# Two mixture routers: a quarter of the side matrices on GpSimd, and group scores through a small network of maxima and minima

## The chip, the cores and the metric

The kernel runs on one core of a Trainium2 chip. The metric is the device time of one execution in microseconds (us). The kernel before was timed three times: 1511.66, 1504.87 and 1511.73 us, median 1511.66 us. One further execution was profiled.

A core has five engines that run their own instruction streams and meet at semaphores: TensorE (PE, with its weight loads as PEld), VectorE (DVE), ScalarE (ACT), GpSimd (POOL) and SyncE (SP, which here only issues DMAs).

## The reference

A two-layer network on 2048 tokens (64 sequences of 32) of width 256. Layer 0: cross attention over a context of 257 rows with 16 heads, a gated linear recurrence (log-space cumulative sums), and a mixture of 8 experts. Layer 1: cross attention, causal self attention, and a mixture of 16 experts. Each part is added to `x` after a layer norm of its input.

The change touches only how the two mixtures choose and place their tokens:

- first mixture: softmax over 8 logits of a token, its 2 best experts;
- second mixture: `sb = sigmoid(logits) + bias` over 16 experts in 4 groups of 4. A group's score is the sum of its two best `sb`; the 2 best groups stay allowed, and the 4 best experts in them are taken.

Then each chosen expert's two-layer network runs on the tokens that chose it, and the weighted results are added to the token.

## The kernel before, in words

Tokens lie as 16 tiles (`NT`) of 128 rows. The program is a row of blocks; at the end of each, all engines meet (a drain and a semaphore exchange, line 1101 in the profile, where the block of a router ends). For each mixture there is: a layer norm block (`boundary`), which also writes the normalised rows to DRAM and computes the logits; the router (`route`, lines 1094 to 1224), called once for each mixture; then the expert tiles (`first_tiles`, `second_tiles`).

`route` makes a table: for each of the NTL tiles of 128 expert rows (39 in the first mixture, 79 in the second) which token stands in each row. In its block:

1. `choose` (on DVE): the scores are ranked. In the second mixture it is the function in `route_second`, lines 2298 to 2332. It takes all six pairs of a group's four `sb` (six additions, line 2306, 64 columns each), and their running maximum (five operations, line 2310, each waiting for the one before); then come the groups' ranks (lines 2317 on) and the 8 best experts (`top8`).
2. Counting (DVE, two matmuls): from the one-hot choices, each token's place within its expert, and from these its row, split into its low 7 bits `lo_f` and a tile threshold `hi_f` (lines 1166 to 1207). All of it is one chain on DVE, nearly every step waiting for the one before.
3. The placing loop (lines 1133 to 1138, 1145 to 1149, 1209 to 1214). It has K times 16 units (32 in the first mixture, 64 in the second). For a unit `u`, DVE makes `hot_lo` (128x128, f16): a row's column is compared with `lo_f` and multiplied by the token's number (tensor_scalar with two operands per partition). ACT makes `side` (128 x NTL+1, f16): the Sign of the column's number plus `hi_f`, so -1 before the tile and +1 from it on. PE multiplies the two and adds up over the 16 units of a choice in PSUM. Both matrices have a ring of 8 buffers; a maker of unit `u` waits until PE has placed unit `u`-8 (`m_placed`), and PE waits for `m_onehot` and `m_side` of its unit.
4. The end: ACT halves the sums (line 1151), DVE subtracts neighbouring columns, which leaves the token's number in its tile alone, and writes `r.token`.

POOL has no instruction in the router's block before the change. SP issues the fetch of the remaining expert weights there (line 980). POOL's next work is in the block behind: gathers of token rows by `r.token` (`gather`, lines 1443 and 1682); the second mixture issues 44 of them (R-4) ahead of its first scatter.

## Time and profile before

| what | us |
|---|---|
| median of three runs | 1511.66 |
| lowest, highest | 1504.87, 1511.73 |
| profiled execution, its own time | 1497.39 |
| its span (first to last instruction) | 1495.6 |
| PE, DVE, ACT, POOL busy | 1160.9, 1026.2, 822.4, 436.4 |
| granted TensorE clock, mean share | 0.889 |
| first router's block, DVE from 539.88 to 558.92 | 19.0 |
| second router's block, DVE from 1109.35 to 1151.13 | 41.8 |

The profiled execution stands 14.3 us under the median of the runs. 1.8 us of its time lie outside the span. PE is the busiest engine over the whole, but a share over the whole says little of a stage: in the routers' blocks PE waits most of the time. In a row of the timeline a merged piece "x64" has the start of the first and the time from there to the end of the last.

### The profile page before, as it was taken

The numbers are of one execution on the slowest core, as the hardware profiler recorded it, in microseconds if no ns is written. First come the engines' busy times: TensorE is split into PE (matmuls) and PEld (weight loads), VectorE is DVE, ScalarE is ACT, GpSimd is POOL, SyncE is SP. The second block draws the span as 40 slices with busy tenths as digits, with TensorE's granted clock in tenths as the row PEclk, the third lists the DMA queues.
The fourth block names the chain that finished last, engine by engine and source line by source line (L and its number), as shares of the span: only waits on it lengthen the run. The fifth ranks groups of instructions, "written<-read, shape, count | busy, mean of one in ns | idle before, by whom it ended". The sixth has DMA issues, their size and how long they took to land. (4 is left out here: it accounts for less than half of the span.)

```text
span 1495.6 us, 41196 instructions
## 1 busy us (share of the span) xinstructions
PE 1160.9 (78%) x13430; PEld 857.0 (57%) x13430; DVE 1026.2 (69%) x2880; ACT 822.4 (55%) x2156; POOL 436.4 (29%) x480
## 2 busy tenths in 40 slices
PE   4899999998699549999999936877936137777780
PEld 2688787886446439988888723334722124555560
DVE  5699999997746888966666545544587168455466
ACT  6688888886588567844443406116455144444450
POOL 0555555552110000023333201100201721555650
PEclk9999999999899759999999967988955578999995
DMA  3333333332000266011111159980063310222228
GB/s 97 97 81 78 81 81 78 82 78 61 23 1 0 70 256 251 2 62 48 48 52 52 38 175 343 315 273 25 1 229 144 102 37 22 80 73 75 81 71 286
DMA packets 111935, 151.45 MB, mean 101 GB/s; under 512 B 13632, under 2 KB 96960, under 8 KB 111680
## 3 DMA queue, kind: packets, MB, share of 16 engines
q1 hardware_dynamic: 95792, 114.11, 24.3%
q0 software_dynamic: 11328, 30.95, 6.6%
q10 hardware_dynamic: 4688, 4.72, 1.0%
q8 instruction: 78, 1.28, 0.4%
q14 instruction: 49, 0.40, 0.1%
HBM read 127.97 MB, written 21.76 MB: 100 GB/s over the span
## 5 line engine op out<-in xcount | busy, mean ns | idle before, releaser
L1359 ACT ACTIVATE mixture_and_attentions_h<-ps,mixture_and_attentions_b 128x128 f32<-128x128 f32 x440 | 124.8, 372 | 136.7 <-PE ps L1307 132.5
L1307 PE MATMUL ps<-xture_and_attentions_m_w 128*128 128x128 f16 x1872 | 155.7, 219 | 1.7 <-DVE xture_and_attentions_m_w L1387 1.7
L1307 PEld LDWEIGHTS ps<-xture_and_attentions_m_w 128*128 x1872 | 129.1, 98 | 36.4 <-issue 2.9
L679 POOL TENSOR_TENSOR ads_and_recurrence_ctx_s<-ads_and_recurrence_ctx_c,ads_and_recurrence_ctx_s 128x512 f16<-128x512 f32 x64 | 74.1, 1158 | 177.7 <-ACT ads_and_recurrence_ctx_s L608 177.7
L1325 PE MATMUL ps<-xture_and_attentions_m_w,ixture_and_attentions_hs 128*128 x312 | 117.4, 379 | 1.0 <-DVE xture_and_attentions_m_w L1413 1.0
L628 ACT ACTIVATE ads_and_recurrence_probs<-ps,s_and_recurrence_neg_max 128x257 f32<-128x257 f32 x256 | 117.6, 479 | 1.1 <-DVE s_and_recurrence_neg_max L710 1.1
L1686 POOL DMA_INDIRECT y_rows<-stage_second_mixture_y,ge_second_mixture_r_dest x79 | 77.1, 975 | 128.8 <-DVE stage_second_mixture_y L1648 115.2
L1682 POOL DMA_INDIRECT tage_second_mixture_rows<-n_rows,e_second_mixture_r_token x79 | 77.1, 975 | 111.6 <-POOLq L1101 87.8
L1443 POOL DMA_INDIRECT ture_and_attentions_rows<-n_rows,e_and_attentions_r_token x39 | 39.2, 1006 | 240.9 <-POOLq L1101 142.4
L1550 PE MATMUL ps<-stage_second_mixture_m_w,stage_second_mixture_x_s 128*128 x474 | 95.1, 339 | 15.7 <-issue 7.1
L1395 DVE TENSOR_SCALAR ixture_and_attentions_hs<-mixture_and_attentions_h 128x512 f16<-128x512 f32 x110 | 47.5, 432 | 81.2 <-PE ps L1326 70.5
L1627 DVE SCALAR_TENSOR_TENSOR stage_second_mixture_h<-ps,stage_second_mixture_h 128x192 f32<-128x192 f32 x95 | 33.7, 355 | 98.1 <-ACT stage_second_mixture_h L1599 60.6
L1565 PE MATMUL ps<-stage_second_mixture_m_w,stage_second_mixture_h_t 128*128 (+1 forms) x95 | 27.0, 285 | 78.0 <-DVE x_sb L1644 36.2
L719 DVE TENSOR_SCALAR _heads_and_recurrence_pn<-ads_and_recurrence_probs,heads_and_recurrence_inv 128x256 f32<-128x256 f32 x256 | 79.7, 371 | 8.3
L1326 PE MATMUL ps<-xture_and_attentions_m_w,ixture_and_attentions_hs 128*128 x312 | 85.0, 273 | 0.0
L710 DVE TENSOR_REDUCE s_and_recurrence_neg_max<-ps 128x2 f32<-128x514 f32 x128 | 81.9, 678 | 1.2 <-PE ps L550 1.2
L525 PE MATMUL ps<-ads_and_recurrence_ctx_s,currence_wh_L_xattn_wk_t 128*128 128x256 f16 x512 | 78.3, 276 | 5.2 <-issue 5.2
L1599 ACT ACTIVATE stage_second_mixture_h<-ps 128x192 f32<-128x192 f32 x95 | 31.5, 331 | 92.3 <-PE ps L1550 45.4
L1397 DVE SCALAR_TENSOR_TENSOR ixture_and_attentions_hs<-mixture_and_attentions_h,ixture_and_attentions_hs 128x512 f16<-128x512 f32 x110 | 76.3, 693 | 3.8
L558 PE MATMUL ps<-consts_sb,_heads_and_recurrence_pn 128*128 128x128 f32 x512 | 77.0, 273 | 2.2 <-DVE heads_and_recurrence_p_t L726 2.2
L534 PE MATMUL ps<-currence_wh_L_xattn_wv_t,ads_and_recurrence_ctx_s 128*128 128x256 f16 x512 | 77.3, 274 | 0.0
L1447 POOL DMA_INDIRECT y_rows<-xture_and_attentions_m_w,re_and_attentions_r_dest x39 | 38.4, 985 | 131.5 <-DVE xture_and_attentions_m_w L1413 131.2
(408 smaller groups left out, 3355.0 us busy)
## 6 DMA issues: line engine op xcount, KB each, us to landing
ads_and_recurrence_ctx_t<-in_ctx_t SPq DMA_DIRECT2D x64, 257.0 KB, 2.7
e_and_attentions_b_ctx_t<-in_ctx_t SPq DMA_DIRECT2D x15, 1028.0 KB, 9.3
ure_and_attentions_b_ctx<-in_ctx SPq DMA_DIRECT2D x30, 512.0 KB, 8.6
xture_and_attentions_m_w<-in_m_w SPq DMA_DIRECT2D x2, 5632.0 KB, 37.9
ds_and_recurrence_mask_i<-in_mask SPq DMA_DIRECT2D x256, 32.1 KB, 1.7
tage_second_mixture_rows<-y_rows SPq DMA_DIRECT2D x16, 512.0 KB, 9.6
stage_second_mixture_m_w<-in_m_w SPq DMA_DIRECT2D x2, 3840.0 KB, 19.3
xture_and_attentions_m_w<-in_m_w SPq DMA_DIRECT2D x1, 5120.0 KB, 15.4
```

Of the source, the lines that this page charges most:

```text
L525: last = pe.matmul(ps[:, KB, m * KR:(m + 1) * KR], w[:, c, m * P:(m + 1) * P], x[:, c, :], start=(n_ == 0), stop=(n_ == len(products) - 1))
L534: last = pe.matmul(ps[:, VB, r * D:(r + 1) * D], x[:, c, r * P:(r + 1) * P], w[:, c, :], start=(n_ == 0), stop=(n_ == len(products) - 1))
L628: act.activation(probs[p][:, j, :], ps[:, SB + j, 0:SK], ACT.Exp, bias=neg_max[:, p, j:j + 1], accum_out=sums[:, p, j:j + 1]).then_inc(k.a ...
L710: dve.tensor_reduce(neg_max[:, p, 2 * h:2 * h + 2], ps[:, SB + 2 * h:SB + 2 * h + 2, 0:SK], AX.X, ALU.max, negate=True).then_inc(k.a_max.s ...
L719: last = dve.tensor_scalar(pn[p][:, j, :], probs[p][:, j, 0:KR], inv[:, p, j:j + 1], None, ALU.mult)
L1307: last = pe.matmul(ps[:, UB + 2 * (u % 2) + f // PER, (f % PER) * P:(f % PER + 1) * P], slots.of(e, c, at, P), a[:, c, :], start=(n == 0), ...
L1325: pe.matmul(ps[:, YB + u % 2, 0:2 * D], h, slots.of(e, block, at, 2 * D), start=(f == 0), stop=False)
L1326: last = pe.matmul(ps[:, YB + u % 2, 0:D], l, slots.of(e, block, at, D), start=False, stop=(f == FC - 1))
L1359: last = act.activation(h32[n][:, at:at + P], ps[:, UB + 2 * (u % 2) + n, at:at + P], ACT.Silu, scale=1 / (WS * NS), bias=b1[:, bass.ds(e ...
L1550: last = pe.matmul(ps[:, UB + u % 2, 0:UP], a[:, c, :], weight(u, w, c * UP, UP), start=(n == 0), stop=(n == len(products) - 1))
L1682: pool.indirect_dma_start(rows[s % R][:, :], None, k.n_rows, bass.IndirectOffsetOnAxis(ap=r.token[:, s:s + 1], axis=0)).then_inc(k.t_rows[ ...
L1686: pool.indirect_dma_start(k.y_rows, bass.IndirectOffsetOnAxis(ap=r.dest[:, s:s + 1], axis=0), y[s % Y], None).then_inc(k.t_stored[s % Y].s ...
```

## The change

- In the placing loop, units 3, 7, 11, ... (a quarter: 8 of 32, 16 of 64) get their `side` from POOL instead of ACT, as 0 or 1 instead of -1 or +1: `(column + hi_f) > 0`, a tensor_scalar with one operand per partition. Their `hot_lo` is multiplied by twice the token's number instead, so that the later halving still fits. A new small table `twice` (16 columns) is made on DVE ahead of `choose`. PE waits for `m_fourth` on these units.
- In `choose` of the second mixture, the 6 additions and 5 maxima become 2 operations of 128 columns (maxima and minima of the first and the second two of a group), 3 of 64 columns, and 2 more of 64 columns, each waiting for the one before; there are 4 waits instead of 6.
- The semaphore `m_counted` is gone; its one increment goes to `m_known`, whose later thresholds rise by one. No other order changes.

```diff
+        twice = k.sb("twice", [P, NT], ctx=ctx)
+        def of_pool(u):
+            return u % 4 == 3
...
-                    pe.wait_ge(k.m_side.sem, k.m_side.at(u + 1))
+                    if of_pool(u):
+                        pe.wait_ge(k.m_fourth.sem, k.m_fourth.at(u // 4 + 1))
+                    else:
+                        pe.wait_ge(k.m_side.sem, k.m_side.at(u + 1 - u // 4))
...
+                    if of_pool(u):
+                        continue
                     act.wait_ge(k.m_placed.sem, k.m_placed.at(u - AHEAD + 1))
                     act.activation(side[u % AHEAD][:, :], iota_h[:, 0:NTS], ACT.Sign, bias=hi_f[:, kk, t:t + 1]).then_inc(k.m_side.sem, 1)
...
+        @block.gpsimd
+        def _(pool):
+            pool.wait_ge(k.m_known.sem, k.m_known.at(2))
+            for u in range(3, K * NT, 4):
+                kk, t = divmod(u, NT)
+                pool.wait_ge(k.m_placed.sem, k.m_placed.at(u - AHEAD + 1))
+                pool.tensor_scalar(side[u % AHEAD][:, :], iota_h[:, 0:NTS], hi_f[:, kk, t:t + 1], 0.0, ALU.add, ALU.is_gt).then_inc(k.m_fourth.sem, 1)
...
+            dve.tensor_scalar(twice[:, :], c_["token"], 2.0, None, ALU.mult)
             choose(dve)
...
-                    dve.tensor_scalar(hot_lo[u % AHEAD][:, :], iota_h[:, :], lo_f[:, kk, t:t + 1], c_["token"][:, t:t + 1], ALU.is_equal, ALU.mult).then_inc(k.m_onehot.sem, 1)
+                    dve.tensor_scalar(hot_lo[u % AHEAD][:, :], iota_h[:, :], lo_f[:, kk, t:t + 1], twice[:, t:t + 1] if of_pool(u) else c_["token"][:, t:t + 1], ALU.is_equal, ALU.mult).then_inc(k.m_onehot.sem, 1)
...
-            pairs = [(a, b) for a in range(EG) for b in range(a + 1, EG)]
-            for n, (a, b) in enumerate(pairs):
-                last = dve.tensor_tensor(pair[:, n, :, :], sb[:, :, :, a], sb[:, :, :, b], ALU.add)
-            last.then_inc(k.m_chain.sem, 1)
-            dve.wait_ge(k.m_chain.sem, k.m_chain.next())
-            for n in range(1, len(pairs)):
-                dve.tensor_tensor(pair[:, 0, :, :], pair[:, 0, :, :], pair[:, n, :, :], ALU.max).then_inc(k.m_chain.sem, 1)
-                dve.wait_ge(k.m_chain.sem, k.m_chain.next())
+            first, second = sb[:, :, :, 0:2], sb[:, :, :, 2:4]
+            dve.tensor_tensor(more[:, :, :, :], first, second, ALU.max)
+            dve.tensor_tensor(less[:, :, :, :], first, second, ALU.min).then_inc(k.m_chain.sem, 1)
+            dve.wait_ge(k.m_chain.sem, k.m_chain.next())
+            dve.tensor_tensor(pair[:, 1, :, :], more[:, :, :, 0], more[:, :, :, 1], ALU.min)
+            dve.tensor_tensor(pair[:, 2, :, :], less[:, :, :, 0], less[:, :, :, 1], ALU.max)
+            dve.tensor_tensor(pair[:, 3, :, :], more[:, :, :, 0], more[:, :, :, 1], ALU.max).then_inc(k.m_chain.sem, 1)
+            dve.wait_ge(k.m_chain.sem, k.m_chain.next())
+            dve.tensor_tensor(pair[:, 4, :, :], pair[:, 1, :, :], pair[:, 2, :, :], ALU.max).then_inc(k.m_chain.sem, 1)
+            dve.wait_ge(k.m_chain.sem, k.m_chain.next())
+            dve.tensor_tensor(pair[:, 0, :, :], pair[:, 3, :, :], pair[:, 4, :, :], ALU.add).then_inc(k.m_chain.sem, 1)
```

## Rows read from the trace of the kernel before

**Rows 1.** The page's first part: busy time, share, instructions of each engine.
```profile
PE 1160.9 (78%) x13430; PEld 857.0 (57%) x13430; DVE 1026.2 (69%) x2880; ACT 822.4 (55%) x2156; POOL 436.4 (29%) x480
```
**Rows 2.** Windows: stretch, length, busy (PE, PEld, DVE, ACT, POOL), clock, DMA share, GB/s.
```profile
550.40:558.00 7.60, 6.49 (x32) 3.33 (x32) 7.21 (x32) 7.14 (x33) 0.00 (x0) 0.50 1.02 409
1132.60:1149.20 16.60, 14.40 (x64) 6.68 (x64) 14.92 (x64) 16.21 (x64) 0.00 (x0) 0.50 0.04 14
```
**Rows 3.** Timeline, second router, scores: start, length, engine, line, operation.
```profile
1110.98 0.42 DVE L2301 TENSOR_TENSOR age_second_mixture_sbias<-stage_second_mixture_y,ixture_w_L_ffn_gate_bias 128x256 f32<-128x256 f32 x1 [1.15 <-ACT stage_second_mixture_y L2296]
1111.44 1.17 DVE L2306 TENSOR_TENSOR tage_second_mixture_pair<-age_second_mixture_sbias 128x64 f32<-128x64 f32 x6
1112.65 1.26 DVE L2310 TENSOR_TENSOR tage_second_mixture_pair<-tage_second_mixture_pair 128x64 f32<-128x64 f32 x5
1113.94 0.42 DVE L2317 TENSOR_TENSOR tage_second_mixture_rank<-tage_second_mixture_pair 128x256 f32<-128x256 f32 x1
```
**Rows 4.** Timeline, second router, the whole placing loop on ACT and DVE.
```profile
1132.61 16.21 ACT L1149 ACTIVATE tage_second_mixture_side<-ge_second_mixture_iota_h,tage_second_mixture_hi_f 128x80 f16<-128x80 f16 x64 [21.56 <-DVE tage_second_mixture_hi_f L1207]
1132.61 14.92 DVE L1214 TENSOR_SCALAR ge_second_mixture_hot_lo<-ge_second_mixture_iota_h,tage_second_mixture_lo_f,consts_sb 128x128 f16<-128x128 f16 x64
```
**Rows 5.** Timeline, the same loop: DVE in its first and last units.
```profile
1132.61 1.65 DVE L1214 TENSOR_SCALAR ge_second_mixture_hot_lo<-ge_second_mixture_iota_h,tage_second_mixture_lo_f,consts_sb 128x128 f16<-128x128 f16 x7
...
1146.71 0.82 DVE L1214 TENSOR_SCALAR ge_second_mixture_hot_lo<-ge_second_mixture_iota_h,tage_second_mixture_lo_f,consts_sb 128x128 f16<-128x128 f16 x3
```
**Rows 6.** Timeline, first router: scores, counting, placing loop, the next block's start.
```profile
540.15 0.28 DVE L1793 TENSOR_SCALAR ixture_and_attentions_lg<-ps 128x128 f32<-128x128 f32 x1
...
545.18 0.29 DVE L1169 TENSOR_TENSOR xture_and_attentions_tmp<-xture_and_attentions_hot 128x128 f32<-128x128 f32 x1
545.51 0.23 DVE L1174 CAST ure_and_attentions_any_h<-xture_and_attentions_tmp 128x128 f16<-128x128 f32 x1
...
547.00 0.17 DVE L1182 TENSOR_SCALAR re_and_attentions_need_i<-ture_and_attentions_upto 128x8 int32<-128x8 f32 x1
...
550.38 7.08 ACT L1149 ACTIVATE ture_and_attentions_side<-re_and_attentions_iota_h,ture_and_attentions_hi_f 128x40 f16<-128x40 f16 x32 [4.05 <-DVE ture_and_attentions_hi_f L1207]
550.39 7.23 DVE L1214 TENSOR_SCALAR re_and_attentions_hot_lo<-re_and_attentions_iota_h,ture_and_attentions_lo_f,consts_sb 128x128 f16<-128x128 f16 x32
...
559.23 6.98 PE L1307 MATMUL ps<-n,xture_and_attentions_m_w 128*128 128x128 f16 x93 [1.34 <-PEq L1101]
```
**Rows 7.** Groups by shape, POOL: busy us, mean ns | idle before.
```profile
L673 POOL TENSOR_SCALAR ds_and_recurrence_mask_b<-ds_and_recurrence_mask_i 128x257 bf16<-128x257 int32 x64 | 70.1, 1096 | 5.4
L672 POOL TENSOR_TENSOR ads_and_recurrence_q_blk<-heads_and_recurrence_q_t,consts_sb 128x128 f32<-128x128 f32 x64 | 29.1, 455 | 0.0
...
L2144 POOL TENSOR_TENSOR x_sb<-x_sb,d_attentions_w_L_attn_bv 128x256 f32<-128x256 f32 x16 | 11.0, 726 | 111.4 <-SPq L2140 111.4
```
**Rows 8.** Single lines, DVE tensor_scalar forms: min/median/max ns, first and last start.
```profile
L2226 DVE TENSOR_SCALAR ture_and_attentions_c_pn<-e_and_attentions_c_probs,ure_and_attentions_c_inv x16: 277/278/845, 1055.3 to 1081.0; 128x128 f32<-128x128 f32 x16
...
L719 DVE TENSOR_SCALAR _heads_and_recurrence_pn<-ads_and_recurrence_probs,heads_and_recurrence_inv x256: 332/342/571, 52.0 to 363.8; 128x256 f32<-128x256 f32 x128
...
L343 DVE TENSOR_SCALAR ads_and_recurrence_ln_xn<-x_sb,s_and_recurrence_ln_mean,ads_and_recurrence_ln_sd x32: 395/397/412, 9.5 to 402.5; 128x256 f32<-128x256 f32 x32
...
L1214 DVE TENSOR_SCALAR ge_second_mixture_hot_lo<-ge_second_mixture_iota_h,tage_second_mixture_lo_f,consts_sb x64: 303/308/316, 1132.6 to 1147.2; 128x128 f16<-128x128 f16 x64
```
**Rows 9.** Timeline, DVE's tensor_scalar of line 2226 beside POOL's bias additions.
```profile
1054.63 2.78 POOL L2144 TENSOR_TENSOR x_sb<-x_sb,d_attentions_w_L_attn_bv 128x256 f32<-128x256 f32 x4
...
1055.28 0.84 DVE L2226 TENSOR_SCALAR ture_and_attentions_c_pn<-e_and_attentions_c_probs,ure_and_attentions_c_inv 128x128 f32<-128x128 f32 x1
```
**Rows 10.** Timeline behind the second router: first and last of the 44 gathers, PE.
```profile
1152.06 0.99 POOL L1682 DMA_INDIRECT tage_second_mixture_rows<-n_rows,e_second_mixture_r_token  x1 [87.83 <-POOLq L1101]
...
1206.66 0.95 POOL L1682 DMA_INDIRECT tage_second_mixture_rows<-n_rows,e_second_mixture_r_token  x1 [0.30 <-issue]
...
1214.31 0.40 PE L1565 MATMUL ps<-stage_second_mixture_m_w,stage_second_mixture_h_t 128*128 128x256 f16 x1 [32.21 <-DVE x_sb L1644]
```

More of the change, by code:

```diff
@@ L1143, in _ @@
             act.activation(warm[:, :], k.ident_h[:, 0:1], ACT.Sign)
-            act.wait_ge(k.m_known.sem, k.m_known.at(1))
+            act.wait_ge(k.m_known.sem, k.m_known.at(2))
             for kk in range(K):
@@ L1221, in _ @@
             dve.tensor_scalar(r.token[:, :], row_f[:, :], 1.0, 0.0, ALU.subtract, ALU.max)
-    for s, n in ((k.m_logits, 1), (k.m_counted, 1),
-                 (k.m_prefixed, 1), (k.m_onehot, NT * K), (k.m_placed, NT * K), (k.m_side, NT * K), (k.m_halved, 1), (k.m_shift, 1), (k.m_expd, 1)):
+    for s, n in ((k.m_logits, 1),
+                 (k.m_prefixed, 1), (k.m_onehot, NT * K), (k.m_placed, NT * K), (k.m_side, NT * K - NT * K // 4), (k.m_fourth, NT * K // 4), (k.m_halved, 1), (k.m_shift, 1), (k.m_expd, 1)):
         s.base += n
@@ L1351, in silu @@
                 if u == NT:
-                    act.wait_ge(k.m_known.sem, k.m_known.at(2))
+                    act.wait_ge(k.m_known.sem, k.m_known.at(3))
                 e = mix.E if u < NT else routed.of(u - NT)
@@ L1450, in _ @@
                 gather(s)
-            pool.wait_ge(k.m_known.sem, k.m_known.at(3))
+            pool.wait_ge(k.m_known.sem, k.m_known.at(4))
             for s in range(mix.tiles):
@@ L1467, in first_tiles @@
         k.t_rows[b].base += (mix.tiles + R - 1 - b) // R
-    k.m_known.base += 3
+    k.m_known.base += 4
     slots.finish()
@@ L1582, in _ @@
                 if u + 4 == NT:
-                    pe.wait_ge(k.m_known.sem, k.m_known.at(2))
+                    pe.wait_ge(k.m_known.sem, k.m_known.at(3))
                 if u + 4 >= NT:
@@ L1693, in _ @@
                 if s == 0:
-                    pool.wait_ge(k.m_known.sem, k.m_known.at(3))
+                    pool.wait_ge(k.m_known.sem, k.m_known.at(4))
                 scatter(s)
@@ L2284, in route_second @@
         sb = k.sb("sbias", [P, NT, NG, EG], ctx=ctx)
-        pair = k.sb("pair", [P, 6, NT, NG], ctx=ctx)
+        pair = k.sb("pair", [P, 5, NT, NG], ctx=ctx)
+        more, less = (k.sb(n, [P, NT, NG, 2], ctx=ctx) for n in ("more", "less"))
         rank = k.sb("rank", [P, 3, NT, NG * NG], ctx=ctx)
@@ L2439, in build @@
         k.m_logits = k.count("m_logits")
-        k.m_counted = k.count("m_counted")
         k.m_prefixed = k.count("m_prefixed")
@@ L2444, in build @@
         k.m_side = k.count("m_side")
+        k.m_fourth = k.count("m_fourth")
         k.m_known = k.count("m_known")
```

10 lines of the change are left out of this document (5 added, 5 removed).

## The prediction

> **What bounds the kernel now.** I read the page's busy shares first [rows 1]: PE is busy 78% of the span, so most stages are PE's, but the change lies in the two stretches where PE hardly works. There I took the windows [rows 2] and then the timeline of each router.
>
> The second router's block is a chain on DVE up to the placing loop. The scores begin at 1110.98, after DVE has waited 1.15 us for ACT, and pass through the six additions and five maxima to the ranks at 1113.94 without a gap [rows 3]. So each microsecond saved there is one saved on the path.
>
> In the placing loop three engines run in step: the question is which sets the pitch. In the second router ACT's 64 units take 16.21 us: less the last one's 0.35, over 63 steps, a pitch of 0.252 us. DVE's 64 take 14.92 [rows 4], and that is not one pitch: its first seven take 1.65, so (1.65 - 0.31)/6 = 0.223 us, its last three 0.82, so 0.253 us [rows 5]. DVE runs ahead until its ring of 8 is full, and from there goes at the pace of PE, which goes at ACT's. ACT is the bound, DVE has 0.029 us a unit to spare. In the first router ACT's matrix is only 40 wide: ACT (7.08 - 0.31)/31 = 0.218 us, DVE (7.23 - 0.31)/31 = 0.223 us [rows 6]. There DVE is the bound already, and taking work from ACT frees nothing.
>
> What follows each router takes a shift whole. PE starts at 559.23 behind the first, with 93 matmuls in one piece [rows 6]. Behind the second POOL issues 44 gathers from 1152.06 to 1207.6, and PE, after 32.21 us of idle time, goes on only at 1214.31 [rows 10]. I read this long stall as tied to the burst of gathers, whose start is the router's end: it moves with the router and hides nothing. A fixed point in it that would swallow a gain, such as the landing of the weights fetched at the block's start, I don't see: the loop's window shows the DMA engines 4% busy [rows 2], so the 9 MB asked for before it have landed.
>
> **The change, part by part.** The sum is made against the profiled execution: span 1495.6, its time 1497.39.
>
> *Scores of the groups (second router only).* Removed: from 1111.44 to 1113.94, 2.50 us [rows 3]. Added: two operations of 128 columns. The pitch of independent 64-column ones is (1.17 - 0.26)/5 = 0.18 us [rows 3], with 64 more columns about 0.25; one that the next waits for costs 0.33 at 128 columns (545.18 to 545.51 [rows 6]). So 0.25 + 0.33 = 0.58. Three of 64 columns: 0.18 + 0.18 + 0.29 = 0.65. Two in a chain at the pitch of line 2310, (1113.94 - 1112.65)/5 = 0.26 us: 0.52. Sum 1.75, a saving of 0.75 us. Bounds: 0.55, if pairs of adjacent columns cost what awkward operands do, and 0.9.
>
> *The table `twice`.* In the second router DVE has 1.15 us of idle time there, so nothing. In the first, `choose` starts at 540.15 with no wait ahead of it: 16 columns at most the 0.17 us of line 1182, back to back rather less: +0.1 us [rows 3, 6].
>
> *ACT's quarter moved.* ACT does 3 units of 4, 3 x 0.252 = 0.76 us per four, under DVE's 4 x 0.223 = 0.89. If POOL's share cost nothing, the second router's loop would be DVE's: 63 x (0.252 - 0.223) = 1.8 us less. The first: nothing.
>
> *What POOL's operation costs.* Its form is not in the trace. POOL's tensor_tensor takes 0.455 us at 128 columns and 0.726 at 256, a slope of 2.1 ns and 0.19 fixed; its only tensor_scalar takes 1.10 at 257 columns, with the same fixed part 3.5 ns a column [rows 7]. For 80 columns that is 0.36 or 0.47, for 40 columns 0.27 or 0.33; the ceiling is the whole 1.10. I take 0.47 and 0.33, by the row of its own kind. POOL has 0.89 us for each, and may begin when the unit 8 before is placed, 1.8 us ahead of need. So POOL itself is in time, also for unit 63, which is POOL's and the last.
>
> *What POOL's operation does to DVE.* This decides the sign. DVE's tensor_scalar of line 2226 takes 0.278 us in the median of 16, and up to 0.845 in those beside POOL's bias additions [rows 8]. In one, DVE's starts at 1055.28 and lasts 0.84, until just after the POOL operation that began 0.03 later has ended (POOL's pitch there is (2.78 - 0.73)/3 = 0.68) [rows 9]. So this kind of DVE operation stands still while POOL runs, and `hot_lo` is of this kind: 256 columns of float32 cost 64 ns more than 128 (0.342 against 0.278), half of what they cost a tensor_tensor (0.42 against 0.29 [rows 3, 6]), and a second operand per partition 55 ns more (0.397). By these a 128-column float32 form with two operands would take 0.333; `hot_lo`, in f16, takes 0.308, so it goes at that double rate or a higher one [rows 8]. How much a POOL operation of length d takes from DVE: where it begins just behind DVE's, 0.845 - 0.278 = 0.57 of 0.72, so d - 0.155. Where it begins anywhere in DVE's period of 0.223 us, a part of that lies beside DVE's own work: on the mean over the period about half of 0.223 less, d - 0.27; and the start and end of a short one, which hold nothing, weigh more, so I take d - 0.30. That is 0.17 us at d = 0.47 and 0.03 at 0.33.
>
> *Sum of the loops.* Second router: 63 x 0.223 = 14.05 for DVE alone, plus 15.75 x 0.17 = 2.7, makes 16.7, against 15.9 (63 x 0.252) before: +0.9 us. The break-even is 0.115 us per POOL operation. First: 7.75 x 0.03 = +0.2 us. All together: +0.9 + 0.2 + 0.1 - 0.75 = **+0.4 us**, 0.03%.
>
> The Trainium skill, "SBUF — State Buffer", section "SBUF: two separate sides", says that VectorE in a mode that uses both of its ports and GpSimd take a shared port pair as an exclusive lock, held for the whole instruction, the other being blocked entirely. The stretched rows of line 2226 agree in kind (0.278 to 0.845 [rows 8]). Read to the letter, the rule gives rival C at its full length, +7.5 us; the row shows 0.57 lost of 0.72.
>
> **The rivals.**
>
> *A, the wash (forecast):* as above, -1 to +2 us.
>
> *B, POOL lies beside DVE at no cost.* For it: most POOL and DVE operations in the trace overlap without a change; a POOL operation of 0.36 us could fit in the gaps between DVE's. Then -1.8 + 0.1 - 0.75 = -2.4 us. Against it: [rows 8, 9].
>
> *C, the slower side: each POOL operation stops DVE for most of its length.* Place: `hot_lo` in both loops; price: d - 0.155, so 0.315 and 0.175 us, for DVE always has the next one waiting. It decides from 0.115 us on. 15.75 x (0.893 + 0.315) - 15.9 = +3.1 us, first router 7.75 x 0.175 = +1.4, with the rest +3.9 us. If DVE loses all of POOL's length, 15.75 x 0.47 + 7.75 x 0.33 = 10.0 us stand in place of A's 2.9: +7.5 us. If POOL's operation costs the ceiling of 1.10, DVE's four and POOL's one in turn give 4 x 0.223 + 1.10 - 0.16 = 1.83 us per four: +13 us in the second, +7.3 in the first, +19.6 in all. I give this far end little.
>
> *D, the burst behind the second router falls otherwise.* PE comes out of it at 1214.31, 6.7 us behind the last gather's issue [rows 10]. I don't know what delays it, so a shift against it can let a tile more or fewer through. PE's idle piece of 32.21 us longer or shorter by a tenth or two is 3 to 6 us either way.
>
> The change doing less than it says is in A and C: in the first router it takes work from an engine that isn't the bound.
>
> **How the numbers follow.** Chances: A 0.47, B 0.18, C 0.23 (0.05 of it DVE losing all of POOL's length, 0.03 the far end), D 0.12. But for those two parts of C, all are below 0.5% of the time (7.5 us), about what a measurement of this kernel can tell from no change, since its own three runs lie 0.45% apart. To this I add that the medians themselves may wander by as much: faster 0.20, same 0.61, slower 0.19. The time: the median 1511.66 + 0.4 is 1512.1. The other executions seen, 1504.87 and 1497.39, lie below, none above 1511.73, so the next median is rather lower: I take 1511.0. The range: upwards C's 3.9 and some of its upper parts, or D, over 1511.7, 1520; downwards B or D from the lower runs (1504.87 - 2.4, less a part of the way to 1497.4), 1499.
>
> **What would show it.** The six-and-five group replaced by 1.75 us, the ranks starting 0.75 earlier. In the second loop: ACT's pieces with gaps (no longer the bound), DVE's `hot_lo` with one in four stretched by about 0.17 us, POOL's operations 0.47 long at a pitch of 1.06, the loop about 16.7 us on DVE. The first loop 7.1 us instead of 6.9. B shows as `hot_lo` at 0.308 throughout and a loop of 14 us; C as stretched ones of 0.62 and a loop over 18 us. The burst must still last 55.6 us and PE resume 62 us after its start; if not, D. The prediction is wrong if POOL's operation lasts near 1 us, if ACT's start waits for POOL's ring, or if the whole moves by over 0.5% by something outside both routers.

## The result: 3 to 4 us faster, and the profile after

The changed kernel takes 1499.92 us in the median of 16 executions (1478.22 to 1503.76), the kernel before 1503.87 beside it (16 executions, 1500.40 to 1511.73): 3.95 us less. The ratio of the comparison is 0.993, 95% interval 0.9904 to 0.9956. Forecast was 1511.0 with 0.61 on no difference. The ratio shows a larger gain than the medians (3.95 us are 0.26%), because it leaves out executions more than 1.5% above the lowest of their kernel: two of the changed kernel's came out near 1480, so its seven over 1500.4 fall away, and none of the kernel before. The medians are the better guide.

The page of the profiled execution after (1502.55 us, span 1500.8), first part:

```profile
span 1500.8 us, 41196 instructions
PE 1168.7 (78%) x13430; PEld 859.3 (57%) x13430; DVE 1027.1 (68%) x2878; ACT 818.8 (55%) x2132; POOL 452.3 (30%) x504
```

Against [rows 1], ACT has 24 instructions fewer (8 and 16 side matrices) and POOL 24 more. This execution is longer than the profiled one of before, 1495.6, although both routers' stretches together are shorter: the first router begins 3.5 us later than before and the second another 3.4, nearly all of it in work that the change doesn't touch (0.3 of the 3.4 is the first router's own). Two single profiles can't be subtracted; stretches of them can.

Windows of the two placing loops after, which answer to [rows 2]:

```profile
554.00:561.80 7.80, 6.72 (x32) 3.33 (x32) 7.38 (x32) 5.84 (x25) 3.61 (x8) 0.50 1.03 411
1138.50:1153.50 15.00, 14.19 (x64) 6.65 (x64) 14.48 (x65) 13.14 (x49) 9.74 (x16) 0.50 0.11 43
```

The scores, on DVE, answering to [rows 3]:

```profile
1117.89 0.42 DVE L2321 TENSOR_TENSOR age_second_mixture_sbias<-stage_second_mixture_y,ixture_w_L_ffn_gate_bias 128x256 f32<-128x256 f32 x1 [1.07 <-ACT stage_second_mixture_y L2316]
1118.35 0.29 DVE L2325 TENSOR_TENSOR tage_second_mixture_more<-age_second_mixture_sbias 128x128 f32<-128x128 f32 x1
1118.55 0.28 DVE L2326 TENSOR_TENSOR tage_second_mixture_less<-age_second_mixture_sbias 128x128 f32<-128x128 f32 x1
1118.87 0.23 DVE L2328 TENSOR_TENSOR tage_second_mixture_pair<-tage_second_mixture_more 128x64 f32<-128x64 f32 x1
1119.02 0.22 DVE L2329 TENSOR_TENSOR tage_second_mixture_pair<-tage_second_mixture_less 128x64 f32<-128x64 f32 x1
1119.15 0.21 DVE L2330 TENSOR_TENSOR tage_second_mixture_pair<-tage_second_mixture_more 128x64 f32<-128x64 f32 x1
1119.40 0.22 DVE L2332 TENSOR_TENSOR tage_second_mixture_pair<-tage_second_mixture_pair 128x64 f32<-128x64 f32 x1
...
1119.92 0.43 DVE L2341 TENSOR_TENSOR tage_second_mixture_rank<-tage_second_mixture_pair 128x256 f32<-128x256 f32 x1
```

From `sbias` to the ranks it is 2.03 us instead of 2.96: -0.93. From start to start, the first of 128 columns costs 0.20, the second 0.32, and the three of 64 columns 0.15, 0.13 and 0.25.

The single lines of `hot_lo` on DVE and of the side matrices on POOL after (min/median/max ns, first and last start), which answer to [rows 8]:

```profile
L1233 DVE TENSOR_SCALAR ge_second_mixture_hot_lo<-ge_second_mixture_iota_h,tage_second_mixture_lo_f,consts_sb x48: 296/298/328, 1138.6 to 1152.5; 128x128 f16<-128x128 f16 x48
...
L1233 DVE TENSOR_SCALAR ge_second_mixture_hot_lo<-ge_second_mixture_iota_h,tage_second_mixture_lo_f,age_second_mixture_twice x16: 296/298/354, 1139.3 to 1152.7; 128x128 f16<-128x128 f16 x16
```
```profile
L1173 POOL TENSOR_SCALAR tage_second_mixture_side<-ge_second_mixture_iota_h,tage_second_mixture_hi_f x16: 551/612/617, 1138.6 to 1151.6; 128x80 f16<-128x80 f16 x16
L1173 POOL TENSOR_SCALAR ture_and_attentions_side<-re_and_attentions_iota_h,ture_and_attentions_hi_f x8: 437/448/537, 554.0 to 559.9; 128x40 f16<-128x40 f16 x8
```

POOL's operation is longer than priced (0.61, not 0.47 us), and `hot_lo` hardly feels it: median 0.298 us, the worst 0.354. In the loop's first two groups of four and then in its steady state the timeline shows this:

```profile
1138.64 1.15 POOL L1173 TENSOR_SCALAR tage_second_mixture_side<-ge_second_mixture_iota_h,tage_second_mixture_hi_f 128x80 f16<-128x80 f16 x2 [67.49 <-DVE tage_second_mixture_hi_f L1226]
1139.25 0.35 DVE L1233 TENSOR_SCALAR ge_second_mixture_hot_lo<-ge_second_mixture_iota_h,tage_second_mixture_lo_f,age_second_mixture_twice 128x128 f16<-128x128 f16 x1
...
1141.82 0.61 POOL L1173 TENSOR_SCALAR tage_second_mixture_side<-ge_second_mixture_iota_h,tage_second_mixture_hi_f 128x80 f16<-128x80 f16 x1 [0.28 <-PE ps L1146]
1142.01 0.30 DVE L1233 TENSOR_SCALAR ge_second_mixture_hot_lo<-ge_second_mixture_iota_h,tage_second_mixture_lo_f,age_second_mixture_twice 128x128 f16<-128x128 f16 x1
1142.23 0.74 DVE L1233 TENSOR_SCALAR ge_second_mixture_hot_lo<-ge_second_mixture_iota_h,tage_second_mixture_lo_f,consts_sb 128x128 f16<-128x128 f16 x3
1142.71 0.61 POOL L1173 TENSOR_SCALAR tage_second_mixture_side<-ge_second_mixture_iota_h,tage_second_mixture_hi_f 128x80 f16<-128x80 f16 x1 [0.28 <-PE ps L1146]
1142.90 0.30 DVE L1233 TENSOR_SCALAR ge_second_mixture_hot_lo<-ge_second_mixture_iota_h,tage_second_mixture_lo_f,age_second_mixture_twice 128x128 f16<-128x128 f16 x1
```

From one `hot_lo` of POOL's units to the next it is 0.89 us, four steps of 0.223: DVE's free pace, with POOL at work in 0.61 of each 0.89. POOL's stretch of waiting (0.28 us, for PE) says that it isn't the bound. The loop, from the start of PE's first matmul to the start of its last, takes 13.99 us instead of 15.85: -1.86. The first router's takes 7.02 instead of 6.81: +0.21. `twice` costs 0.08 (543.635 to 543.712, the next operation's start). From `sbias` to gather 0 the second router takes 38.33 us instead of 41.08, -2.75. So the stretches give -2.75 + 0.21 + 0.08 = **-2.5 us**, where rival B said -2.4.

### The profile page after: what moved, and what is told of

Read it like the earlier page. It is cut to its first block and busy times, and to the rows that moved or that the text cites. A ratio compares the mean times of both kernels' runs of the same rounds, so it can differ in the third digit from the quotient of the medians.

```text
span 1500.8 us, 41196 instructions
## 1 busy us (share of the span) xinstructions
PE 1168.7 (78%) x13430; PEld 859.3 (57%) x13430; DVE 1027.1 (68%) x2878; ACT 818.8 (55%) x2132; POOL 452.3 (30%) x504
## 5 line engine op out<-in xcount | busy, mean ns | idle before, releaser
L1613 ACT ACTIVATE stage_second_mixture_x_s<-ps 128x512 f16<-128x512 f16 x79 | 47.3, 599 | 46.7 <-PE ps L1557 36.5
## 6 DMA issues: line engine op xcount, KB each, us to landing
xture_and_attentions_m_w<-in_m_w SPq DMA_DIRECT2D x1, 5120.0 KB, 15.6
```

## The experiments

Theory: the change is worth what its stretches show (-2.5 us), since POOL's operation costs DVE next to nothing. Rivals: the larger ratio is real and comes from what lies behind the router; POOL does stop DVE, and something hides it.

**The parts alone, the change and the kernel before once more.** Four kernels on one chip, the kernel before beside them (median 1498.92 us, 35 executions). The loops alone keep the six additions and five maxima:

```diff
-            first, second = sb[:, :, :, 0:2], sb[:, :, :, 2:4]
-            dve.tensor_tensor(more[:, :, :, :], first, second, ALU.max)
...
+            for n, (a, b) in enumerate(pairs):
+                last = dve.tensor_tensor(pair[:, n, :, :], sb[:, :, :, a], sb[:, :, :, b], ALU.add)
...
```

> The placing loops of the change alone, the group scores as before. Path theory (what a router saves is what the kernel saves): second loop, first to last matmul, 14.0 us instead of 15.9, first loop 7.0 instead of 6.8, group scores 2.95 as before; time 1.7 us under before, 0.1%. Burst theory (the change also alters how the 44 gathers' stall falls, and that gives the executions near 1480): single executions 15 to 25 us under the rest appear here too if POOL's new instructions are the cause.

The scores alone are the reverse.

> The network of maxima and minima alone, all side matrices on ACT. Path theory: 0.9 us from the first score to the ranks less than before, loops as before, time 0.9 us less. Burst theory: executions near 1480 only if a shift of the router's end, or another number of DVE instructions, is the cause; none if POOL's instructions are.

> The changed kernel once more. Path theory: median 2.6 us under before (router 2: 0.9 + 1.9, router 1: 0.2 back), 0.17%. Burst theory: again some executions (2 or 3 of 16) near 1480, and the mean 5 us or more under before; if there are none here, those seen were chance of the chip and not of the change.

> A copy of the kernel before, to see how far two sets of executions of one program differ. Both theories: median within 1.5 us of before's. If it shows executions near 1480 as well, these belong to both kernels. Its second trace tells how much the stretch from the second router's end to the last of 17 weight casts (91.0 us in the first trace) wanders by itself: under 1 us if it is set by the gathers alone, several if PE's stall in it is a matter of chance.

Later the change, the loops alone and the scores alone ran again, with the kernel before at 1504.82 (35 executions).

> The changed kernel, unaltered. One of two surroundings is possible: one in which the kernel before takes 1495 to 1505 us and PE pauses through the second mixture, or the one of the last four runs, in which it takes 1406.8 us and PE is full there. In either, the theory that the change is worth what its own stretches show (second loop -1.86, scores -0.93, first loop +0.2) expects -2.6 us: about 1404.2 beside 1406.8, or 1498 beside 1500.5, ratio 0.998. The rival, that the -10 us in the ratio of the first comparison is real and comes from what the mixture does with an earlier or later start, expects -8 to -12 us, 0.993.

> The kernel before with the part of the change in the loops alone (the scores as before). Own stretches: second loop -1.86, first loop +0.2, so -1.7 us. Rival: that this part by itself makes runs near 1475 us (4 of 12 in the first look), by 20 us, expects those again wherever the kernel before takes about 1500; where it takes 1407 there is no pause to lose, and both theories say -1.7.

> The kernel before with the network of the scores alone. Own stretch: -0.93 us (2.03 instead of 2.96 from sbias to rank). If that is all, the whole is 1 us less, within what can be told from nothing. Rival (what the router gives is lost behind it): 0.

Measured (medians in us; stretches from each kernel's profile):

```
                       median  beside before    sbias to ranks  loop 2  sbias to gather 0  loop 1
kernel before (trace)                             2.96          15.85      41.08            6.81
loops alone            1494.35     -4.57          2.96          14.00      39.27            7.04
loops alone, again     1500.32     -4.50          2.96          13.97      39.24            7.05
scores alone           1499.99     +1.07          2.04          15.85      40.16            6.81
scores alone, again    1505.10     +0.28          2.04          15.85      40.17            6.81
the change, again      1496.24     -2.68          2.03          14.01      38.36            7.03
the change, third      1501.16     -3.66          2.04          13.97      38.32            7.04
before, again          1500.45     +1.53          2.96          15.85      41.10            6.81
```

These stretches repeat to 0.05 us and add up: each part does what it does alone. The medians don't: the loops alone gain 3.0 us more than their stretches (1.5), twice, and the scores come out 1.2 to 2.0 worse than theirs (0.9). The kernel before against itself is off by 1.53 (one of those twelve executions took 1850.14 us; without it the median is 1500.42), so one such difference means little. That the loops came out alike twice stays open: the second time no execution lay apart, and the ratio, 0.9962 with an interval of 0.9943 to 0.9982, leaves out the 0.999 that their stretches give.

What wanders lies outside the routers. From gather 0 to the last scatter the two traces of the kernel before take 305.7 and 296.1 us, and from gather 0 to the last weight cast 91.0 and 79.4; the expectation had asked for under 1 us if the gathers alone set that stretch. The traces of the change and its parts beside them lie between 299 and 308 us. So ten microseconds can come and go there in one unaltered kernel, which is what rival D feared, and more than it priced (3 to 6).

A group of executions near 1475 us adds to the wander: 8 of the 88 of all kernels with a part of the change, none of the 98 of the kernel before (lowest 1489.82); none lies between 1481.38 and 1489.82. No profile fell on one of them. Their cause isn't known.

**Does POOL stop DVE?** In the kernel before, a two-input operation of POOL beside the loops, whose result nobody reads:

```diff
+        spare = k.sb("spare", [P, NT * K // 4 + 1, NTS], F16, ctx=ctx)
...
+        @block.gpsimd
+        def _(pool):
+            pool.wait_ge(k.m_known.sem, k.m_known.at(1))
+            for u in range(3, K * NT, 4):
+                pool.wait_ge(k.m_placed.sem, k.m_placed.at(u - AHEAD + 1))
+                pool.tensor_tensor(spare[:, u // 4, :], iota_h[:, 0:NTS], iota_h[:, 1:NTS + 1], ALU.subtract)
```

> The kernel before, with one thing added: in the loop over 0/1 matrices GpSimd subtracts, at every fourth step, two slices of iota_h (128x40 in the first router, 128x80 in the second, two fp16 inputs) into a tile that nobody reads. Nobody waits for it and ACT still makes every side matrix, so whatever it does to DVE's hot_lo is the pair's doing alone. If two-input operations of GpSimd are what stops DVE (the theory, from L2226 stretched beside a tensor_tensor in rows 8 and 9, while the one-input operation of the change left hot_lo at 0.297 us): the hot_lo that lies beside one is stretched by about as much as the GpSimd operation lasts, 0.4 to 0.6 us, four steps of DVE take 0.9 + 0.4 to 0.6 = 1.3 to 1.5 us against ACT's 1.0, and the second loop lasts 20 to 24 us instead of 15.85; whole time +5 to +8 us with both routers. If a short DVE operation on fp16 isn't stopped by GpSimd whatever that reads: hot_lo stays under 0.35 us, the loop lasts 15.9 us, whole time within 1 us.

Measured: 1406.13 against 1406.77 (that these are some 95 us lower is taken up below), ratio 1.0003 (0.9987 to 1.002). The single lines and the loop on ACT:

```profile
L1222 DVE TENSOR_SCALAR ge_second_mixture_hot_lo<-ge_second_mixture_iota_h,tage_second_mixture_lo_f,consts_sb x64: 298/302/433, 1133.7 to 1149.6; 128x128 f16<-128x128 f16 x64
L1159 POOL TENSOR_TENSOR age_second_mixture_spare<-ge_second_mixture_iota_h x16: 319/320/321, 1133.8 to 1148.4; 128x80 f16<-128x80 f16 x16
1133.73 16.21 ACT L1150 ACTIVATE tage_second_mixture_side<-ge_second_mixture_iota_h,tage_second_mixture_hi_f 128x80 f16<-128x80 f16 x64 [21.56 <-DVE tage_second_mixture_hi_f L1215]
```

One `hot_lo` that is held, by itself, and the POOL operation beside it:

```profile
1143.31 0.41 DVE L1222 TENSOR_SCALAR ge_second_mixture_hot_lo<-ge_second_mixture_iota_h,tage_second_mixture_lo_f,consts_sb 128x128 f16<-128x128 f16 x1
1143.35 0.32 POOL L1159 TENSOR_TENSOR age_second_mixture_spare<-ge_second_mixture_iota_h 128x80 f16<-128x80 f16 x1 [0.68 <-PE ps L1139]
```

The time went as the second theory had it, the operation as the first, if by 0.11 us and not 0.4 to 0.6: DVE stands until POOL's two-input operation is through. All 16 held ones of the second router end 0.047 to 0.050 us after POOL's operation, as all six stretched ones of line 2226 in the trace before [rows 8, 9] end 0.084 to 0.086 after theirs. So the price isn't fixed. The next `hot_lo` starts 0.031 us ahead of POOL's end, and the loss is POOL's length plus its start behind `hot_lo`'s, less 0.254: 0.114 where POOL (0.320) begins 0.048 behind, 0.131 where it begins 0.065 behind, 0.044 beside the first, 0.256 us long, of the first router. Five of the first router's eight (0.253 us) begin 0.21 behind a `hot_lo`, end in time for the next, and cost nothing.

Why doesn't the loop feel it? The steady state's four steps are 3 x 0.223 + 0.337 = 1.006 us, and ACT's are 4 x 0.252 = 1.007. My reading, not tested, is that this is no accident: POOL's start is released by PE, which goes at ACT's pace, so if DVE gets ahead, POOL starts later behind `hot_lo` and holds it longer. The loop stays at 15.85 and the total doesn't move. ACT's slack hides the loss here; beside a loop that DVE bounds, as the changed one, a two-input operation was not tried.

**POOL without rest: every second matrix.** `u % 2 == 1` in place of `u % 4 == 3`, and the counts to match.

> The changed kernel with GpSimd making every second side matrix instead of every fourth. DVE at 0.223 us a step is what bounds the changed loop (13.99 us for 63 steps in the second router). If GpSimd's own pace is the limit of sharing: its operation takes 0.61 us with some 0.05 us until the next, two steps take 0.66 us, the second loop lasts 31 x 0.66 = 20 to 21 us and the first, with 0.45 us an operation, about 16 x 0.5 = 8 us; whole time +6 to +8 us over the changed kernel. If GpSimd stops DVE more, the more of its time it works, DVE's hot_lo is stretched too, above 0.35 us for most. If GpSimd had kept pace, both loops would stay at 14.0 and 7.0 us and the whole within 1 us.

Measured 1407.82 against 1406.77 (+1.05; ratio 0.9999 to 1.0024). Single lines, second router:

```profile
L1233 DVE TENSOR_SCALAR ge_second_mixture_hot_lo<-ge_second_mixture_iota_h,tage_second_mixture_lo_f,consts_sb x32: 305/312/317, 1134.9 to 1151.3; 128x128 f16<-128x128 f16 x32
L1233 DVE TENSOR_SCALAR ge_second_mixture_hot_lo<-ge_second_mixture_iota_h,tage_second_mixture_lo_f,age_second_mixture_twice x32: 308/389/394, 1135.2 to 1151.6; 128x128 f16<-128x128 f16 x32
L1173 POOL TENSOR_SCALAR tage_second_mixture_side<-ge_second_mixture_iota_h,tage_second_mixture_hi_f x32: 544/547/607, 1135.0 to 1151.6; 128x80 f16<-128x80 f16 x32
```

The loop takes 16.84 us, not 20: back to back POOL's operation is 0.547 long and its pitch 0.533. Every second `hot_lo` is 0.39 long and its step 0.310, 0.087 lost. The first loop takes 6.89. The expected +6 to +8 us over the changed kernel didn't come, since that would be at least +3.5 over the kernel before. The expected 0.61 + 0.05 had taken for the operation's own length what was in part a wait inside it.

This is the counterpart to the two-input operation. A held `hot_lo` and the POOL operation beside it, which began 0.02 later:

```profile
1144.11 0.39 DVE L1233 TENSOR_SCALAR ge_second_mixture_hot_lo<-ge_second_mixture_iota_h,tage_second_mixture_lo_f,age_second_mixture_twice 128x128 f16<-128x128 f16 x1
1144.13 0.55 POOL L1173 TENSOR_SCALAR tage_second_mixture_side<-ge_second_mixture_iota_h,tage_second_mixture_hi_f 128x80 f16<-128x80 f16 x1
```

`hot_lo` ends 0.37 us after POOL's start, with 0.18 of POOL's operation still to come, and DVE goes on beside the rest. The change's own operation (tensor_scalar, one input) holds DVE for a first part only, where the tensor_tensor with two inputs holds it to its end. The two differ in the operation and in the number of inputs; which of these matters wasn't separated.

**The second router alone, other units, every third.** One line in each (with the counts to match):

```diff
-            return u % 4 == 3
+            return NT * K == 64 and u % 4 == 3        # second router alone
+            return u % 4 == 1                         # other units
+            return u % 3 == 2                         # every third
```

> The changed kernel with GpSimd's side matrices in the second router alone; the first router's loop is as before (ACT makes all 32). By the stretches: the first loop goes back from 7.02 to 6.81 us, so 0.2 us better than the changed kernel, -2.8 us under the kernel before; that can't be told from the change as a whole in time, only in the trace. Rival: with the first router undisturbed the executions near 1475 us are as many or as few.

> GpSimd's side matrices in the second router alone, once more, for its trace. If the pattern (GpSimd operations of 0.556 and 0.624 us in turn, hot_lo stretched to 0.405 beside the short ones, 14.62 us from PE's first to its last) belongs to this kernel, it is there again; if it is an accident of one execution, the loop takes 14.0 us as in the changed kernel.

> The changed kernel with GpSimd making the side matrices of units 1, 5, 9 and so on instead of 3, 7, 11. The work is the same; only where its operations begin against DVE's shifts, since each is released by PE's unit 8 before it. If the loss depends on who comes first: either the 14.0 us of the changed kernel (GpSimd's operations 0.61 long, hot_lo 0.30) or a part of the units blocked by 0.10 each, up to 14.0 + 1.6 = 15.6 us, GpSimd's operations then 0.555. A mixed figure would be a blocked hot_lo beside a GpSimd operation of 0.61.

> The changed kernel with every third side matrix made by GpSimd. Its operation of 0.55 to 0.61 us fits under three steps of DVE (0.669), so GpSimd is not the bound: second loop 14.0 us if DVE loses nothing, up to 14.0 + 21 x 0.10 = 16.1 us if each GpSimd operation takes 0.10 from DVE. No gain over every fourth is possible, DVE being the bound there.

Measured: the second router alone 1403.25 against 1407.24, ratio 0.9976 (0.9963 to 0.9988); the change itself beside it 0.9973. Its first loop is back at 6.82 us, but in this profile its second takes 14.62, not 14.0. POOL and DVE there:

```profile
1134.55 0.62 POOL L1173 TENSOR_SCALAR tage_second_mixture_side<-ge_second_mixture_iota_h,tage_second_mixture_hi_f 128x80 f16<-128x80 f16 x1 [0.45 <-PE ps L1146]
1135.43 0.56 POOL L1173 TENSOR_SCALAR tage_second_mixture_side<-ge_second_mixture_iota_h,tage_second_mixture_hi_f 128x80 f16<-128x80 f16 x1 [0.26 <-PE ps L1146]
1136.43 0.62 POOL L1173 TENSOR_SCALAR tage_second_mixture_side<-ge_second_mixture_iota_h,tage_second_mixture_hi_f 128x80 f16<-128x80 f16 x1 [0.45 <-PE ps L1146]
```
```profile
1134.95 0.85 DVE L1233 TENSOR_SCALAR ge_second_mixture_hot_lo<-ge_second_mixture_iota_h,tage_second_mixture_lo_f,consts_sb 128x128 f16<-128x128 f16 x3
1135.72 0.31 DVE L1233 TENSOR_SCALAR ge_second_mixture_hot_lo<-ge_second_mixture_iota_h,tage_second_mixture_lo_f,age_second_mixture_twice 128x128 f16<-128x128 f16 x1
1135.94 0.75 DVE L1233 TENSOR_SCALAR ge_second_mixture_hot_lo<-ge_second_mixture_iota_h,tage_second_mixture_lo_f,consts_sb 128x128 f16<-128x128 f16 x3
```

Three `hot_lo` take 0.75 free and 0.85 beside the short POOL operation. So in the steady state a meeting costs one of the two: either POOL's operation is 0.61 to 0.64 long and DVE's step undisturbed, or POOL's is 0.55 and DVE loses 0.08 to 0.11. In this profile DVE lost in 7 of 16. In another execution of the same kernel it lost in one and the loop took 14.00, so the pattern didn't belong to the kernel. With units 1, 5, 9 it lost in two of 16 (14.06 us), with every third in four of 21 (14.23 us). Who loses isn't told by the phase alone: POOL began 0.033 to 0.039 us after a `hot_lo` in six units where DVE lost, and 0.028 to 0.034 after one in the changed kernel's steady state, where POOL did. The length of `hot_lo` alone doesn't tell: in the second execution it grows from 0.31 to 0.35 us through the loop while its step stays at 0.222. The last three traces are of single executions (1495.90, 1502.43, 1501.80 beside 1507.11), whose times carry no verdict.

Had DVE lost 0.10 in every unit, the loop would take 14.0 + 1.6 = 15.6 us, still under 15.85: at this price, which is that of the change's own operation, the second loop doesn't come out slower.

**Does a router's length reach the end?** Twelve more operations in the second router's `choose`, in the kernel before:

```diff
+            for _ in range(12):
+                dve.tensor_tensor(masked[:, :, :], flat, flat, ALU.add).then_inc(k.m_chain.sem, 1)
+                dve.wait_ge(k.m_chain.sem, k.m_chain.next())
```

> The kernel before with 12 chained additions of 128x256 fp32 put into the second router's choose on DVE, results not used, about 0.46 us each, so 5.5 us. If the second router's chain passes whole to the end (as the sum of the prediction has it): sbias to first gather is 46.6 us instead of 41.1, and the whole time rises by 5 to 6 us. If the burst behind the router takes up what the router gives or loses (rival): less than 2 us of it reach the end.

> The kernel before with 12 chained additions of 128x256 fp32 in the second router's choose on DVE (5.5 us, seen in the trace as sbias to first gather 46.6 instead of 41.1 us). If the length of the router passes whole where PE pauses behind it too: +5.5 us in the median. If the pauses behind it take it up: under +2 us. If any shift of the mixture's start makes executions near 1475 us: 1 or more of 12.

```profile
1114.96 5.48 DVE L2305 TENSOR_TENSOR ge_second_mixture_masked<-age_second_mixture_sbias 128x256 f32<-128x256 f32 x12
```

From `sbias` to gather 0: 46.60 and 46.61 us, +5.5. The whole: ratios 1.0026 (1.0014 to 1.0039) and 1.0035 (1.002 to 1.005), +3.7 and +4.9 us, intervals 2.0 to 5.5 and 2.8 to 7.0. Most of the length reaches the end; both comparisons were made where the kernel takes 1407 us, so for the other surroundings this stays untested.

**The change where nothing pauses.** Two chips ran the kernel before in 1407 us (all runs given above beside 1406.77 or 1407.24); the others ran it in 1499 to 1507. Windows from gather 0 to the last weight cast and from there to the last scatter, for the kernel before at 1500 and for the change at 1407 (columns as in [rows 2]):

```profile
1152.06:1243.08 91.02, 33.70 (x210) 20.38 (x208) 41.98 (x96) 28.87 (x47) 42.45 (x44) 0.68 0.23 64
1243.08:1457.79 214.71, 169.77 (x1435) 123.51 (x1435) 123.47 (x427) 100.78 (x238) 110.70 (x113) 0.94 0.22 70
```
```profile
1154.37:1200.50 46.13, 32.35 (x210) 19.77 (x208) 41.57 (x95) 28.53 (x47) 36.37 (x33) 0.87 0.32 89
1200.50:1367.15 166.65, 158.04 (x1435) 119.43 (x1435) 124.08 (x427) 103.63 (x238) 122.85 (x126) 0.96 0.32 100
```

The same 210 and 1435 matmuls take 45 and 48 us less, 93 together, where the spans differ by 90.5. Over both windows DVE's and ACT's busy times are within 2%; PE's is 13 us shorter at 1407, with a higher granted clock in both windows. The rest is waiting. The routers' stretches are as in the table.

> The changed kernel, unaltered. If the change is worth what its stretches show: median 2.6 us under the kernel before. If there are more executions near 1475 us with it than with the kernel before for a reason of its own: 1 or 2 of 12 again, and 0 of 35 in the kernel before. Where the kernel before takes 1407 us, none in either, and -2.6 us plain.

Measured: 1402.51 against 1407.24 (-4.73), ratio 0.9973, 0.996 to 0.9986, so -3.8 us with an interval of -5.6 to -2.0. The stretches' -2.5 lies in it. No execution here lies apart from the rest (1400.96 to 1408.87), so this gain doesn't rest on executions like those near 1475.

**Fewer gathers ahead.** In the changed kernel the burst is cut from 44 to 18:

```diff
-                while gathered < min(R - 4 + (mix.tiles - R + 4) * (s + 1) // (mix.tiles - 20), mix.tiles):
+                while gathered < min(18 + (mix.tiles - 18) * (s + 1) // (mix.tiles - 20), mix.tiles):
```

> The changed kernel with 18 instead of 44 gathers issued ahead of the first scatter in the second mixture; the other gathers follow between the scatters. Theory 'the burst of gathers is the stall': behind the second router the work of all engines stands until GpSimd is through its 44 gathers (54 to 58 us, of which each takes 1.25 us), so with 18 the stall ends some 32 us earlier (gather 0 to the last weight cast 57 us instead of 87 to 91), and the whole time falls by 10 to 30 us, less what later gathers cost between scatters. Rival 'the stall is the weights' DMA': the time from gather 0 to the last weight cast stays at 80 to 90 us and the whole time within 3 us. Third: the gathers are needed that early; then waits for a gathered row appear in the mixture and the time rises by 5 us or more.

> The changed kernel with 18 instead of 44 gathers ahead of the first scatter. Where the kernel before takes 1407 us: +25 us over it again, since the mixture then waits for rows. Where it takes about 1500 us, theory 'the gathers in flight hold up PE's signals': PE's work of the mixture's start, which there stood until 62 us after gather 0, goes on 30 us earlier; the last weight cast comes 60 us after gather 0 instead of 82 to 91, but the later gathers stand between the scatters where they hold up signals too, so the whole is between -20 and +25. Rival 'something else than gathers holds up PE': the last cast stays at 80 to 90 us.

Measured: 1432.26 against 1406.77 (+25.5, four executions), and 1509.91 against 1504.82 (+5.1; against the change beside it +8.7). At 1407 nothing stands behind the burst to be won (45.7 us to the last cast instead of 46.1), and PE waits 18.6 us for gathered rows, which it doesn't in the changed kernel. At 1500, the windows with 18 and, below, with 44:

```profile
1153.20:1215.79 62.59, 35.10 (x210) 20.70 (x208) 41.59 (x95) 28.85 (x47) 18.70 (x19) 0.77 0.14 41
1215.79:1469.45 253.66, 184.48 (x1435) 130.95 (x1435) 122.11 (x427) 100.69 (x238) 135.67 (x138) 0.89 0.23 72
```
```profile
1152.37:1241.22 88.85, 35.87 (x210) 21.40 (x208) 42.47 (x95) 28.86 (x47) 44.50 (x44) 0.69 0.24 66
1241.22:1457.48 216.26, 170.02 (x1435) 123.59 (x1435) 124.22 (x427) 101.17 (x238) 111.48 (x114) 0.94 0.22 69
```

The same 210 matmuls come through 26 us earlier (79.4 to 91.0 us were seen with 44 gathers, 62.6 with 18), and the stretch into which 26 gathers are put off is 37 us longer. PE's last long pause with 18:

```profile
1175.21 0.40 PE L1584 MATMUL ps<-stage_second_mixture_m_w,stage_second_mixture_h_t 128*128 128x256 f16 x1 [11.75 <-issue]
```

It ends 22.0 us behind gather 0 (1153.20), against 62 to 63 with 44 in nearly all traces. So the pause is tied to the gathers, as the prediction read it; what differs between the surroundings is not shown. In the waits of the kernel before at 1500, ACT stands for signals whose sender the profile doesn't show; at 1407 ACT has no such line in any trace, and with 18 gathers at 1500 it still has (26.7 and 20.9 us), so these waits don't go with the burst alone:

```profile
ACT stage_second_mixture_h L1599 <- remote: 19.6, 9, 11.0
ACT stage_second_mixture_h_t L1604 <- remote: 18.5, 6, 6.7
```

## Why the prediction was wrong

**The step that failed: "What POOL's operation does to DVE".** It priced 0.17 us per POOL operation against a break-even of 0.115, and forecast 16.7 us for the second loop. Measured in the changed kernel: 0.053 and 0.026 us in the second and third and nothing from there on; the loop takes 13.99 us, so that the sum's +0.9 for it became -1.86. The error was to carry [rows 8, 9] over to another kind of operation. There a float32 operation of DVE stood through a two-input tensor_tensor of POOL, and for that kind the reading was right: `hot_lo` too stands until such an operation ends. The change's operation is a tensor_scalar of one input. A `hot_lo` that it held ended by 0.37 us after its start (0.39 in one unit each of two traces), with much of its 0.55 to come, so DVE lost 0.11 at most; and in the steady state of the changed kernel it is POOL that waits (0.61 instead of 0.55 us) and DVE loses nothing. What decides which of the two waits stays open. The formula d - 0.30 failed for the other kind also: at d = 0.32 it gives 0.02, and 0.114 was lost. The Trainium skill's rule weighed there ("SBUF — State Buffer", section "SBUF: two separate sides"), an exclusive lock for the whole instruction, agrees with the runs for POOL's two-input operation (held to its end in all 16 of the second router) and not for the change's one-input operation: 0 to 0.11 us lost beside 0.55 to 0.61.

**POOL's length** was mis-sized too: 0.55 back to back, and 0.61 with the wait in it, for 0.47, and 0.45 for 0.33, from the slope of its nearest kinds. By the formula d - 0.30 the lengths of 0.61 and 0.45 would have moved the forecast to 0.4 + 15.75 x 0.14 + 7.75 x 0.12 = +3.5 us, further off: a better length could not have mended the wrong mechanism.

**The bound after the change** was right: DVE at 0.223, 63 steps, 14.05 us; ACT's quarter was worth the 1.8 us stated. The first loop came out at +0.21 for +0.2, by luck: 0.03 a unit was the formula's value for a length of 0.33, and for the 0.45 that POOL took it gives 0.15, while the trace shows 0.03 in four units and 0.07 in one. `twice` was right (0.08 for 0.1). **The scores** gave 0.93 for 0.75, outside the bound of 0.9: the independent 128-column one cost 0.20 and not 0.25, and the pitch of three independent ones, with the dependent end, 0.53 and not 0.65.

**The burst** (rival D): first to last gather takes 56.25 us (1156.22 to 1212.47) against 54.60, and PE's last long pause ends 62.8 us behind gather 0 against 62.3. In this trace it moved with the router, as said. In the second trace of the kernel before, the pauses within it sum to less (79.4 us to the last cast for 91.0), so D's effect exists without the change and hides in the medians.

**The 0.5% bound.** Rival B, at -2.4 us, was put under "same", being 0.16%. By mechanism that was right: the stretches give -2.5. But the comparisons gave 0.993 here, 0.9945 and 0.9973 later, with intervals below 1 (and once 0.9991, whose interval holds 1). With 12 to 16 executions, and 25 or 35 of the kernel before, 3 to 4 us can be told where no executions lie apart, which the three runs shown didn't suggest. What lies between -2.5 and the medians' -2.7 to -4.7 is the wander of medians (the kernel before against itself: 1.5), and, in the ratio, executions near 1475 us whose cause stays open. The absolute time was 11 us too high, since it started from 1511.66; the kernel before came out at 1503.87. That 1499.92 still lies above the lower bound of 1499 is due to the width given for the runs' wander, and says nothing for the sum.

## What to carry to other kernels

Where two engines share a loop, work out the break-even of what the one takes from the other, and before carrying a stretched pair over from the rows, ask whether it is of the same kind as yours. Here a two-input operation of POOL held DVE until its end, and the one-input operation of the change cost a tenth of a microsecond at most, paid by either side. That made a third engine's help nearly free until the next engine's own pace (DVE, 0.223 us a step) was reached; every third matrix gave nothing over every fourth, and every second made POOL the bound. And compare the touched stretches of traces before totals: the routers' repeat to 0.05 us (but for one loop of 14.62 against 14.00 in the same kernel), where medians of a dozen executions wander by 1.5 and the stretch behind the second router by 10.

## What the runs showed of the hardware that was not expected

- A DVE tensor_scalar (`hot_lo`, fp16) that meets a POOL tensor_tensor with two fp16 inputs (0.320 us) stands until 0.048 us after POOL's end, 16 times of 16; beside a POOL tensor_scalar with one input (0.547 us) a held one ends 0.37 us after POOL's start, with 0.18 us of POOL's operation to come.
- POOL's tensor_scalar on 80 fp16 columns takes 0.547 us back to back (pitch 0.533) and 0.61 to 0.64 when it starts beside a running `hot_lo` that isn't held up: its length in a trace can hold a wait.
- The same program takes 1407 us on some chips and 1500 on others, with the busy times of DVE and ACT in the second mixture within 2%: at 1500 PE and the engines behind it wait while POOL's indirect gathers and scatters are under way. Cutting the gathers ahead from 44 to 18 puts the kernel 25 us over the kernel before on the one and 5 on the other (9 over the change beside it).
